# The beginning of a fused ternary octonion FFN: weights by windows, untransposed, with gate and x on one DMA queue and up on another

## The reference

```python
y    = einsum('bct,bcd->bdt', x, cond_weights[itok])
s    = mean(|W|);  Wq = s * clip(round(W / s), -1, 1)        # for gate, up, down
M    = einsum('jik,jod->koid', S_OCT, Wq)                    # 8 blocks, signed
gate = y @ M_gate;  up = y @ M_up                            # 1024 -> 2728
out  = x + (silu(gate) * up) @ M_down
```

## Time and profile before

| | |
|---|---|
| median of 3 runs | 737.66 us (737.5 to 737.69) |
| profiled execution | 737.88 us |
| its span, first to last instruction | 736.1 us |
| PE busy | 684.5 us, 93% |
| DVE busy | 540.2 us, 73% |
| POOL busy | 371.2 us, 50% |
| ACT busy | 335.2 us, 46% |
| mean granted PE clock | 0.972 of full |

### The profile page before, as it was taken

How to read it: one execution, slowest core, us unless ns; L and a number is a source line. 1 busy time by engine, 2 the same in 40 slices (tenths; PEclk the granted TensorE clock), 3 DMA queues, 4 the chain that set the end, 5 groups by cost and what they waited for, 6 DMA issues and landing times. The chain is left out here.

```text
span 736.1 us, 16887 instructions
## 1 busy us (share of the span) xinstructions
PE 684.5 (93%) x6934; PEld 621.6 (84%) x6934; DVE 540.2 (73%) x852; ACT 335.2 (46%) x529; POOL 371.2 (50%) x426
## 2 busy tenths in 40 slices
PE   3259968999999999999999999999999999999995
PEld 3248957999899998999899998999899998998895
DVE  3868649766877768766886778776786768777877
ACT  4534744445452554435462545434562545434531
POOL 0200897364663357464663357464563447564553
PEclk9659989999999999999999999999999999999999
DMA  8300110021100310020100310020100300011001
GB/s 244 124 1 1 59 61 2 3 89 41 49 1 2 115 62 1 2 87 32 60 2 1 116 61 2 2 86 32 62 1 2 115 2 2 2 63 54 1 2 58
DMA packets 16847, 31.32 MB, mean 43 GB/s; under 512 B 3330, under 2 KB 10498, under 8 KB 16770
## 3 DMA queue, kind: packets, MB, share of 16 engines
q1 hardware_dynamic: 16770, 30.24, 11.9%
HBM read 21.84 MB, written 8.39 MB: 41 GB/s over the span
## 5 line engine op out<-in xcount | busy, mean ns | idle before, releaser
L962 PE MATMUL ps<-y_op,gate_table 128*128 128x256 f16 x2112 | 273.5, 275 | 13.7 <-DVE h_op L797 8.7
L962 PE MATMUL ps<-y_op,up_table 128*128 128x256 f16 x2112 | 272.0, 274 | 2.7 <-DVE up_table L740 2.7
L962 PEld LDWEIGHTS ps<-y_op,gate_table 128*128 128x128 f16 x2112 | 208.2, 99 | 39.8 <-DVE h_op L797 9.2
L962 PEld LDWEIGHTS ps<-y_op,up_table 128*128 128x128 f16 x2112 | 207.6, 98 | 28.0 <-DVE up_table L740 3.2
L520 POOL TENSOR_TENSOR h_pairs<-h_f 128x256 f32<-128x256 f32 (+1 forms) x128 | 119.5, 961 | 99.8 <-ACT h_f L614 96.3
L520 POOL TENSOR_TENSOR z_f<-h_pairs 128x512 f32<-128x512 f32 x80 | 102.5, 1302 | 97.9 <-DVE z_op L802 95.9
L640 ACT ACTIVATE ps<-ps,small 128x512 f32<-128x512 f32 x96 | 63.6, 662 | 164.7 <-DVE ps L815 123.1
L431 POOL TENSOR_TENSOR o_sb<-o_sb,wd_sb 128x256 f32<-128x256 f32 (+1 forms) x150 | 88.2, 624 | 90.9 <-DVE wd_sb L862 89.7
L714 DVE TENSOR_TENSOR pu_sb<-ps,q_sb 128x512 f32<-128x512 f32 x96 | 65.9, 687 | 48.1 <-ACT q_sb L636 29.3
L1039 PE MATMUL ps<-down_c,h_op 128*128 128x128 f16 x1536 | 92.1, 219 | 0.5 <-issue 0.5
L1039 PE MATMUL ps<-down_u,z_op 128*128 128x256 f16 x768 | 90.1, 273 | 1.5 <-DVE z_op L802 1.5
(11 more groups left out here) (76 smaller groups left out, 481.3 us busy)
## 6 DMA issues: line engine op xcount, KB each, us to landing
x_in<-in_x_dram SPq DMA_DIRECT2D x8, 1024.0 KB, 5.3
o_sb<-in_x_dram SPq DMA_DIRECT2D x16, 512.0 KB, 3.5
out_dram<-o_sb SPq DMA_DIRECT2D x15, 512.0 KB, 2.7
h_op<-in_L_ffn_w_gate_dram SPq DMA_DIRECT2D x3, 512.0 KB, 5.4
h_op<-in_L_ffn_w_up_dram SPq DMA_DIRECT2D x3, 512.0 KB, 5.5
z_op<-in_L_ffn_w_down_dram SPq DMA_DIRECT2D x1, 1364.0 KB, 9.2
cond_bd<-in_L_cond_weights_dram SPq DMA_DIRECT2D x32, 16.0 KB, 2.9
out_dram<-o_sb SPq DMA_DIRECT2D x2, 256.0 KB, 2.1
```

Of the source, the lines that this page charges most:

```text
L962: mm = pe.matmul(dst, table[m][:, slot, q, :], y_op[:, op, e, :], start=(i == 0 and e == 0), stop=(i == len(terms) - 1 and e == 1))
```

## The change

The weights now come laid out by windows with the feature dimension of gate and up already on the partitions (the host only pads and permutes), so nothing is transposed on the chip; the last window is padded with zeros instead of overlapping. The work of the beginning is cut into windows. Gate and up have their own ternary values and slots for each window, and eight operations on several blocks at once build a window's 21 slots.

- SP's queue loads gate, x, the condition matrices, down; ACT's queue, ahead of ACT's other work, loads up.
- DVE's order: gate scale; window (gate, 0); y's scales; up scale; h's scales; two pieces of y's low half; window (up, 0); the third piece; chunk 0; the down scales; then as listed below.
- PE runs two x rounds before gate's sum. PE forms `down_u` itself: 12 mixes of 16 products with the identity or its negative, each into the y bank, copied out by ACT. A mix waits for the copy of the one before. They stand at two places of chunks 2 to 7: between shared and own, and behind own.
- ACT has a mix's copy ahead of `split_h` of the chunk before (place 0) or behind silu (place 1).
- Tile 1's x rounds move to chunks 8 to 10, its norms to chunk 11, its scales behind DVE's chunk 11.
- POOL has no work for down any more; the rest of its program, and the places of `z_hi` and `z_lo`, are as before.

```diff
+    Y_AT_FIRST = {(8, 1): 0, (9, 1): 1, (10, 0): 2, (10, 1): 3}
+    NORM_AT_FIRST = (11, 0)
+    TABLES_AFTER = {0: [(0, 1)], 1: [(1, 1)], 4: [(0, 2)], 5: [(1, 2)]}
+    DOWN_AFTER = {0: 0, 1: 1, 2: 2}
+    MIX_AT = [(c, half) for c in range(2, 8) for half in range(2)]
...
             for w in range(NQ):
-                sp.dma_start(raw[0][:, w], w_gate[:, WIN[w]:WIN[w] + P, :].rearrange("j o d -> o j d")
-                             ).then_inc(gate_loaded[w], 16)
+                sp.dma_start(raw[0][w], w_gate[:, w]).then_inc(gate_loaded[w], 16)
             load_x(0)
...
             load_cond(0)
-            for w in range(NQ):
-                sp.dma_start(raw[1][:, w], w_up[:, WIN[w]:WIN[w] + P, :].rearrange("j o d -> o j d")
-                             ).then_inc(up_loaded[w], 16)
-            sp.dma_start(raw_down, w_down.rearrange("j o d -> o j d")).then_inc(down_loaded, 16)
+            sp.dma_start(raw_down_at, w_down.rearrange("p w j o -> p (w j o)")).then_inc(down_loaded, 16)
             load_x(1)
             load_cond(1)
-            sp.wait_ge(transposed, 3 * NQ)
+            sp.wait_ge(down_mixed, len(MIXES))
+            sp.wait_ge(down_c_ready, len(corr))
...
             sum_y(0)
-            down_weights()
             for T in range(NT):
...
+            for w in range(NQ):
+                act.dma_start(raw[1][w], w_up[:, w]).then_inc(up_loaded[w], 16)
             act.wait_ge(ones_set, 1)
...
                     act.activation(q_sb[:], bank_q, ACT.Copy).then_inc(q_copied, 1)
+                if T == 0:
+                    first_tile_at(c, 0)
                 if c > 0:
                     split_h(T, c - 1)
                 act.wait_ge(g_ready, n + 1)
                 act.activation(bank_r(s, 0), bank_r(s, 0), ACT.Silu, scale=gate_scale(T)).then_inc(silu_ready, 1)
+                if T == 0:
+                    first_tile_at(c, 1)
...
+            def mix_out(i):
+                w, h, v = MIXES[i]
+                act.wait_ge(down_mixed, i + 1)
+                act.activation(down_u[:, w, v, :, h, :], bank_mix, ACT.Copy).then_inc(down_u_ready, 1)
...
+            def build_table(m, w):
+                signed_add(to(0, 4), t[:, 0:4], t[:, 4:8], 1).then_inc(built, 1)
+                signed_add(to(4, 4), t[:, 0:4], t[:, 4:8], -1).then_inc(built, 1)
+                signed_add(to(14, 2), t[:, 4:7:2], t[:, 1:8:6], 1).then_inc(built, 1)
+                signed_add(to(16, 2), t[:, 4:7:2], t[:, 1:8:6], -1).then_inc(built, 1)
+                dve.tensor_scalar(to(18, 2), t[:, 4:8:3], 1.0, None, ALU.mult).then_inc(built, 1)
+                dve.tensor_scalar(to(20, 1), t[:, 4:5], -1.0, None, ALU.mult).then_inc(built, 1)
+                dve.wait_ge(built, NBUILD * w + 2)
+                dve.tensor_scalar(to(8, 3), to(1, 3), -1.0, None, ALU.mult).then_inc(built, 1)
+                dve.tensor_scalar(to(11, 3), to(5, 3), -1.0, None, ALU.mult).then_inc(built, 1)
...
                     chunk(T, c)
+                    if T == 0 and c == 0:
+                        scales(2)
+                        scale_of_down()
+                        scale_down(0)
+                    if T == 0 and c in DOWN_AFTER:
+                        w = DOWN_AFTER[c]
+                        ternary(2, w, tern_down[:, w], raw_down[w], next(n_tern))
+                    if T == 0 and c in TABLES_AFTER:
+                        for m, w in TABLES_AFTER[c]:
+                            window_of(m, w)
                     if c in Z_LO_AFTER:
                         z_lo(T, Z_LO_AFTER[c])
...
+            def mix(i):
+                w, h, v = MIXES[i]
+                pe.wait_ge(tern_ready[2], w + 1)
+                if i == 0:
+                    pe.wait_ge(ident_set, 2)
+                    pe.wait_ge(scale_ready, 9)
+                else:
+                    pe.wait_ge(down_u_ready, i)
+                for r in range(4):
+                    for t, (j, sign) in enumerate(mixes[h, v, r]):
+                        mm = pe.matmul(bank_mix[:, r, :], (ident if sign > 0 else minus_ident)[:], tern_down[:, w, j, :],
+                                       start=(r == 0 and t == 0), stop=(t == 3), skip_group_check=True)
+                mm.then_inc(down_mixed, 1)
...
+            def first_tile_at(c, half):
+                if (c, half) in MIX_AT:
+                    mix(MIX_AT.index((c, half)))
+                if (c, half) in Y_AT_FIRST:
+                    y_round(1, Y_AT_FIRST[c, half])
+                if (c, half) == NORM_AT_FIRST:
+                    row_norms(1)
```

More of the change, by code:

```diff
@@ L28 @@
+import itertools
 from contextlib import ExitStack
@@ L189, in build, with both @@
     corr = down_plan()
[L191 to L195, removed]
+    def both(j, a, b):
+        return weight((j, a), (j + 4, b))
+    order = [both(j, 1, 1) for j in range(4)] + [both(j, 1, -1) for j in range(4)]
+    order += [both(j, -1, -1) for j in range(1, 4)] + [both(j, -1, 1) for j in range(1, 4)]
+    order += [weight((1, 1), (4, 1)), weight((6, 1), (7, 1)), weight((1, -1), (4, 1)), weight((6, 1), (7, -1))]
+    order += [weight((4, 1)), weight((7, 1)), weight((4, -1))]
+    slots = {w: n for n, w in enumerate(order)}
+    assert set(slots) == {w[0] for w in [*wr.values(), *wpr.values()]} | set(wq.values())
     NSLOT = len(slots)
+    NBUILD = 8
     xr = x.rearrange("b c t -> (b c) t")
@@ L410, in pair_up @@
             return op
-        g_blocks = []
+        mixes = {}
         for (h, v), f in F_SIGN.items():
@@ L415, in build @@
                 r1, r0 = divmod(r, 2)
[L416 to L420, removed]
+                terms = []
+                for a in range(2):
+                    first = 4 * (h ^ v) + 2 * a
+                    sign = f[2 * a] * (1, parity(r1))[a]
+                    other = parity(r0) if f[2 * a] == f[2 * a + 1] else -parity(r0)
+                    terms += [(first, sign), (first + 1, sign * other)]
+                mixes[h, v, r] = sorted(terms, key=lambda t: -t[1])
+        MIXES = [(w, h, v) for w in range(NQ) for h, v in F_SIGN]
+        assert len(MIXES) == len(MIX_AT)
         def back_to_outputs(eng, s, r0):
@@ L620, in z_hi @@
                     act.wait_ge(z_ready, (NR - 1) * T + k + 1)
[L621 to L627, removed]
-                act.activation(z_op[:, k, 0], z_of(k), ACT.Copy).then_inc(z_hi_ready, 1)
+                if T == 0 and k % 2 == 0:
+                    for m in range(2):
+                        act.wait_ge(slots_built[m], NBUILD * min(NQ, k + 2))
+                    if k > 0:
+                        act.wait_ge(tern_ready[2], NQ)
+                act.activation(z_op[:, k, 0], z_of(k), ACT.Copy).then_inc(z_hi_ready, 1)
+            def first_tile_at(c, half):
+                if (c, half) in MIX_AT:
+                    mix_out(MIX_AT.index((c, half)))
+                if (c, half) in Y_AT_FIRST:
+                    copy_y(1, Y_AT_FIRST[c, half])
             def chunk(T, c):
@@ L865, in mix_down, with window_of @@
                 last.then_inc(wd_ready, 1)
+            n_tern = itertools.count()
+            def window_of(m, w):
+                ternary(m, w, tern[m][w], raw[m][w], next(n_tern))
+                build_table(m, w)
             scales(0)
-            ternary(0, tern[0], raw[0])
-            build_table(0)
+            window_of(0, 0)
+            y_scales(0)
             scales(1)
             scales_of_ffn()
-            scales(2)
-            scale_of_down()
-            ternary(1, tern[1], raw[1])
-            dve.wait_ge(fixed_scales, 3)
-            scales_of_tile(0)
-            y_lo(0)
-            build_table(1)
+            h_scales(0)
+            y_lo(0, range(2))
+            window_of(1, 0)
+            y_lo(0, range(2, NY))
             for T in range(NT):
@@ L1013, in gate_up, with first_tile_at @@
                     shared(T, c)
-                else:
-                    if c % 2 == 0:
-                        shared_pair(T, c)
-                    shared(T, c)
-                    own(T, c)
+                    return
+                if T == 0 and c % 4 == 0:
+                    for m in range(2):
+                        pe.wait_ge(slots_built[m], NBUILD * (c // 4 + 1))
+                if c % 2 == 0:
+                    shared_pair(T, c)
+                shared(T, c)
+                if T == 0:
+                    first_tile_at(c, 0)
+                own(T, c)
+                if T == 0:
+                    first_tile_at(c, 1)
+            def first_tile_at(c, half):
+                if (c, half) in MIX_AT:
+                    mix(MIX_AT.index((c, half)))
+                if (c, half) in Y_AT_FIRST:
+                    y_round(1, Y_AT_FIRST[c, half])
+                if (c, half) == NORM_AT_FIRST:
+                    row_norms(1)
             def down_c_of(w, halves=(0, 1)):
@@ L1146, with in_windows @@
     from concourse.bass_utils import run_bass_kernel_spmd as _run
+    def in_windows(a, axis):
+        n = a.shape[axis]
```

(9 more changed lines are left out.)

275 lines of the change are left out of this document (102 added, 173 removed).

## The result

The changed kernel takes 744.5 us (741.52 to 746.16, 6 runs), the kernel before 737.67 us (737.5 to 737.82, 6 runs): ratio 1.0091, interval 1.0072 to 1.0111. It is slower, by 6.8 us. The profiled execution took 743.76 us, span 741.9.

The account below looks back on a forecast made before the run. PE bounds every tile from tile 1 on; own up starts 18 us earlier, but tile 0 gives it back, DVE being the bound up to mix 2. Tile 1 starts 7.1 later: 737.9 + 7.1 = 745.0, as median 744.8, range 735.5 to 751.

Parts of the forecast that it names:

- Loads: Start of the kernel: queues share equally, x in at 12.8, condition loads hidden behind x, x rounds at 13.1.
- Window (gate, 0): DVE before own: ternary done at 20.0, slots beside POOL's y sums done at 24.3, with 2.2 lost to POOL.
- First add: DVE's first add at 38.5, 5.2 after own up, between 3.9 at full clock and 6.5.
- DVE up to mix 2: Tile 0: DVE is the bound, PE stops 4 for h's low half, mix 2 begins at 61.3.
- The rival in which these windows are covered: DVE between chunks 0 and 2: PE sets chunks 1 to 3, mix 2 at 50.9, time 734.6; chance 0.13.
- Mix 2 to the last y copy: Tile 0 behind mix 2: 50.0 of PE work plus stops and waits, last y copy ready at M + 57.6, 119.0.
- POOL before down: Before down: POOL's y sums precede z round 2, on which ACT waits; PE stops 8.9, plus 1.8 at low clock.
- The rival without this stop: Down does not wait for z round 2: 734.3, needing another order on ACT; chance 0.03.
- SP's queue ahead of ACT's: Loads: x in at 9.1, chain up to mix 2 moves by 3.7, time 741.3, still slower; chance 0.17.
- The lock: DVE windows beside POOL's z rounds: exclusive port lock could lose all of a round, sum about 2.7 higher.
- third rival: Each DVE operation blocks for a whole POOL operation: 0.5 + 2.7, and 2 more where ACT falls behind, 750; chance 0.15.
- went at about half speed and did not stop: The prediction's reading, from the earlier profile, of DVE's slot work beside POOL's five y operations.

Follow-up runs that it names:

- the reduced mixes: Changed kernel with each mix at 4 products instead of 16, three of four terms of each down_u block left out: 742.42 us.
- the version with late windows: Changed kernel with y sums behind z round 3, down's ternaries behind chunks 0, 2, 3, up on SP's queue, windows (gate, 2), (up, 2) behind chunks 5, 6: 725.2 us.
- the version where POOL waits: Changed kernel with POOL's sums of tile 0's y waiting until DVE has built window (gate, 0)'s slots: 744.5 us.
- one queue: Changed kernel with up's three loads on SP's queue, behind the conditions and ahead of down, nothing on ACT's: 741.46 us.

## Why the prediction was right

It gave 744.8, range 735.5 to 751, slower with 0.77; measured were 744.5. The mechanism is the one that the trace shows: an early start, DVE as the bound up to mix 2, and POOL's order ahead of down. That the number came within 0.3 is partly luck. Against the profiled execution (743.76) the sum of 745.0 was 1.2 too high, and the changed kernel's median happens to lie 0.7 above that execution. The stages missed by +1.3 (loads), -0.3 (x rounds to own up), -1.4 (own up to first add), -1.1 (first add to mix 2), -0.5 (POOL ahead of down) and +0.7 (the clock behind that stop), so they partly cancel. Its steps against the trace:

| start, us | predicted | measured |
|---|---|---|
| x rounds | 13.1 | 14.42 |
| own up of chunk 0 | 33.3 | 34.31 |
| DVE's first add | 38.5 | 38.09 |
| mix 2 | 61.3 | 59.80 |
| last y copy ready | 119.0 | 117.4 |
| down | 132.9 | 130.75 |
| tile 1 | 156.0 | 154.51 |

- **Loads.** Equal shares of the two queues were about right: x landed at 13.6 for the 12.8 forecast. But the condition loads, which I let hide behind x, were the ones that released PE. The last was issued at 7.98 and landed 6.3 later, at 14.3; the median over all condition loads of the run is 2.9. Down's load was issued at 8.50; what share of the delay is its, no run shows. Cost: 1.3 in all.
- **Window (gate, 0)** took 21.04 to 24.98, 3.9 for the 4.3 of the prediction, and 5.0 in the execution of the reduced mixes. The forecast had this window on the path. The trace has it just beside: DVE still waited 0.26 for PE's sum of up (25.91), and with the sums of y held back the median did not move. In the other execution DVE did not wait there, and own began 0.8 later.
- **First add.** Own up ran at full clock (1.92), so 3.8 and not 5.2 went by from 34.31: the warm end of the bound.
- **DVE up to mix 2.** Right in mechanism: both stops came, ended by h's low half (3.6 for 4.0) and by ACT's down_u copy (3.0 for 4.9; PE came to it 0.4 later than forecast, at 56.8, for own(2) ran longer at the low clock, and mix 2 began 1.5 earlier). A window takes 3.8, not 4.1: the slot operations of a window 1.7 instead of 2.1. Two windows at 0.3 and a first add 0.4 earlier make 1.0 of the 1.5 by which mix 2 was early. The rival in which these windows are covered falls: moving 2 us of DVE work moved mix 2 by 1.7.
- **Mix 2 to the last y copy.** 57.6 predicted, 57.6 measured, partly by luck. The stop before mix 8 was 3.3 for 2.9, the one before mix 10 did not come (1.4), the small waits were 0.3 in place of 1.2. What replaced them is the low clock after the stop before mix 8, 1.5, which had no term. I called PE the bound here; the reduced mixes show that DVE and ACT are nearly one too.
- **POOL before down.** Right: the chain came out in the order given, 8.3 for 8.9, and the experiment that moves the y sums removes it. The low clock after it cost 2.6, not 1.8. The rival without this stop asked for another order on ACT; the experiment removed the stop by another order on POOL, and gave 733.7 for its 734.3.
- **SP's queue ahead of ACT's** as a rival falls (x rounds at 14.42), and putting up on SP's queue is worth the 3 us that it was priced at (3.7).
- **The lock.** Beside POOL, window (gate, 2) took 3.6 us more (7.4 against 3.8), between the 2.6 of the forecast and the 5.3 (2.6 + 2.7) of its third rival. That DVE's slot work "went at about half speed and did not stop" was read from merged rows and does not hold here. One by one, the first two slot adds began at 78.15 and 79.45 and took 1.37 and 1.49; each ended 0.3 behind POOL's operation of the moment (77.18 to 79.24, 79.20 to 80.65), and alone such an add takes 0.4. The other two met no POOL work and took 0.28 each. POOL waited as well: 2.06 and 1.45 for its two pairs, 1.25 each when DVE leaves it alone. The Trainium skill, SBUF — State Buffer, "SBUF: two separate sides", states that the port pair which the two engines share is locked for a whole instruction and the other engine blocks. The trace agrees. So the third rival (0.15) had the mechanism, and the forecast the nearer size; what the lock costs depends on how many operations meet.

So the 17.0 us of the beginning are gone by tile 1: from own up to tile 1 it is 120.2 now and was 97.6, 22.6 more. The mixes less the transposes are 9.4 of it, and the other 13.2 are, to within 0.5, the stops with the low clock behind them, over what before had of both.

## What to carry to other kernels

When work is moved, look at what an in-order engine has queued behind the new place: here the y sums of POOL, harmless at chunk 7, held z, h and PE at chunk 10, and the place of one step was worth 10.8 us. Price a stop of PE with the restart at the low clock behind it where PE is the bound afterwards, and ask of a saving whether it only makes such a stop longer. A second DMA queue brings no bandwidth where one fills the engines; it changes the order of arrival, so leave on it nothing that competes with what the first engine waits for.

## What I had not expected

The low clock can be a second payment for a stop. After 3.6 idle the 32 products of own(2) took 6.15 from start to start instead of 3.5; after 3.0 the 32 of own(3) took 5.2; after 8.3 down's first 48 took 6.1 instead of 3.5; after 0.9 nothing was lost. It is not paid every time. In the version with late windows and in the one where POOL waits, own(2) ran at 1.92 after the same stop of 3.6 (granted clock 1.00 from 48 to 52 in the latter, 0.50 in the changed kernel), and with one queue own(3) and own(6) ran at full clock after 2.75 and 3.29. And it is paid only where PE is the bound behind it: with own(2) at full clock in the version where POOL waits, mix 2 began at 59.95, no sooner than the 59.80 of the changed kernel, because it waits for DVE and ACT; only the stop before it was longer, 5.63 for 2.99.

A faster PE in the x rounds can also start own later. Five profiled executions have the same program up to there. In three the second two x rounds took 2.84 to 3.02 and own began at 30.50 to 30.78; in two they took 2.07 and 2.12, POOL started sooner, DVE's slot operations beside it took longer (3.30 for 1.16) and own began at 31.19 and 31.26. That is some 0.6 us; what makes the 4.6 us between the changed kernel's runs was not shown.
